# The spectrum steps of a fused four-layer kernel one to a slot, and at its beginning the input tiles ahead of the padded copy

## The chip, the cores and the metric

One core of a Trainium2 chip runs the whole program. The metric is the device time of one execution in microseconds (us), the median of several. Engines are called as the profile calls them: PE (TensorE), DVE (VectorE), ACT (ScalarE), POOL (GpSimd) and SP (SyncE, which here only issues DMAs; POOL issues DMAs too).

## The reference

Sixteen images of 224 x 224 pixels and 32 channels go through four residual layers, `x = x + layer(groupnorm(x))`. Only layers 0 and 1 are touched here.

```python
x = x + _L0_conv_ref(_gn(x), L0_conv_W, L0_conv_b, 224)  # offsets dy, dx = clip(mean(x) @ W + b, 0, 28);
                                                         # the image shifted by (dy, dx), zeros moved in
x = x + _L1_conv_ref(_gn(x), L1_conv_W, L1_conv_b)       # sign(x) * (sum over m of sign(W[m])), 3x3, SAME
x = x + _L2_conv_ref(_gn(x), ...)                        # 32 x 32 Fourier/cosine modes mixed, back, + x @ W.T, relu
x = x + _L3_conv_ref(_gn(x), ...)
```

Layer 2 begins with a cosine transform over columns and a Fourier transform over rows of each image, of which 32 x 32 modes are kept. These forward transforms are already worked out in the pass over layers 0 and 1, and stored in `spec`.

## The kernel before

`shift_conv_forward` does layers 0 and 1 and layer 2's forward transforms. The engines run in order, each its own list, and meet by semaphores only. The order is written out by hand.

Before the loop, image 0 is read in 16 tiles (`load_x`: of each, SP loads the two upper quarters of the partitions and POOL the two lower). DVE turns each tile into the image buffer (`turn_x`), and ACT sums it and its squares (`x_tile`); a ring of 4 tile buffers (`RING`) is between. From the sums come the mean, the variance and the offsets, which SP and POOL read from the tile `offi`. The shifted image is then read with the offset in its address. For image 0 that can reach ahead of the input, so its first 8 shifted tiles are read from `xpad`, a copy of the image's upper part with 29 rows of zeros ahead of it (L353 zeros, L355 copy). `pad_done` counts those DMAs. DVE also prepares the convolution's kernel sums (L722 to L743).

After that, `body(b, ...)` runs for b = -1 to 15, and each engine has its own version of it. A body has 16 slots. In it image b is convolved (`has_v`), image b+1 gets its shifted tiles added (`has_s`), image b+2 is read and its statistics are taken (`has_x`), and the spectrum of image b-1 is finished (`has_tail`). The steps of a slot s are

- PE: `conv(b, s)`, 18 matmuls into one of two PSUM pairs `cps`; `turn_back(b, s-1)`, 8 transposes in two halves into the two banks `aps`; every other slot `forward_cols` (tile `vps`)
- DVE: `add_conv(b, s)` (L846), which waits for the conv and frees its PSUM pair; `turn_x` (L812) for image b+2; `add_shifted` (L823 to L838) for image b+1; now and then `signs` (L870)
- ACT: `copy_back` (L618), the two halves from `aps` to `tout`; `square` (L649); `x_tile` (L600, L606) for each tile that DVE turned one slot earlier, four instructions of two tiles in slots 1 to 3
- SP and POOL: the loads of the tiles, four tiles ahead of DVE.

The spectrum of image b-1 is 8 steps. Step k of `spectrum` on PE is `forward_rows(k-1)` (L535, needs ACT's copy of step k-1) and `turn_spec(k)` (L524, 4 transposes into `aps[k % 2]`). ACT then copies that bank to `colpart` (`copy_cols`, L636). The banks `aps` are shared with `turn_back`: `ring_item` makes PE wait before it writes a bank until ACT has copied what stood in it two items earlier. `ring_t` and `ring_o` number the items of a body. After step 7 ACT copies the result (`copy_spec`) and SP stores it in eight DMAs (`store_spec`). PE's `conv(b, s+1)` stands behind `turn_back(b, s-1)` and slot s's spectrum steps.

A body whose flags are all set runs for b = 1 to 13 (13 bodies, 12 of them in a loop of four turns over three); b = 14 and b = 15 have less of DVE's work.

## Time and profile before

| | us |
|---|---|
| median of 3 runs | 3697.39 (3688.41 to 3705.35) |
| the profiled execution | 3689.45, span of its instructions 3687.8 |
| first tile turned | 60.77 |
| first convolution added (body 0) | 180.5 |
| body 0 | 93.9 |
| bodies 1 to 13 | 1370.1, 105.4 each |
| body 14 | 84.3 |

A body is counted from the first `add_conv` on DVE to the next body's. The profiler's own execution is one of several, and layers 2 and 3 fill the rest of the span. In the rows below a wait stands in brackets or behind a bar, with what ended it.

### The profile page before, as it was taken

What the parts mean: (1) busy time and instruction counts of PE and PEld (TensorE: products, weight loads), DVE (VectorE), ACT (ScalarE), POOL (GpSimd) and SP (SyncE); (2) the same over time, 40 slices, a digit from 0 to 9 for tenths busy, and PEclk for the clock granted to TensorE, in tenths of its full rate; (3) what the DMA queues carried; (4) which work ended last, traced back from release to release, by engine and by line L of the source; (5) the groups of instructions that cost most, each with busy time, mean ns of one, the idle gap of its engine ahead of it and who ended that gap; (6) DMA issues with size and microseconds to landing.
All of it is one profiled execution on the core that took longest, in us unless ns stands there. A gap on an engine that the chain in (4) does not pass through costs nothing. (4 is left out here: it accounts for less than half of the span.)

```text
span 3687.8 us, 59833 instructions
## 1 busy us (share of the span) xinstructions
PE 3025.0 (82%) x17264; PEld 1403.7 (38%) x17264; DVE 2731.0 (74%) x3908; ACT 1507.8 (41%) x2728; POOL 553.4 (15%) x1059
## 2 busy tenths in 40 slices
PE   0189888888899888899847888888888727999997
PEld 0034444443344444444444333333333316444443
DVE  3897887888878788886144776767676642999998
ACT  3476766676767666764352222222222223000000
POOL 2333322233233233321010000000000010000000
PEclk9988887897888888889767999999999857999998
DMA  5676665676676666764176555454545255999998
GB/s 148 174 228 211 203 195 184 205 223 204 204 215 199 185 199 207 223 188 133 70 140 274 235 201 235 200 235 200 236 199 237 114 120 170 343 384 388 386 379 296
DMA packets 255824, 808.76 MB, mean 219 GB/s; under 512 B 85466, under 2 KB 119774, under 8 KB 244724
## 3 DMA queue, kind: packets, MB, share of 16 engines
q1 hardware_dynamic: 163796, 370.64, 30.8%
q10 hardware_dynamic: 58368, 316.72, 22.0%
q0 software_dynamic: 33376, 118.13, 11.3%
q8 instruction: 115, 1.88, 0.2%
q14 instruction: 169, 1.38, 0.1%
HBM read 479.39 MB, written 329.56 MB: 219 GB/s over the span
## 5 line engine op out<-in xcount | busy, mean ns | idle before, releaser
L969 POOL DMA_DIRECT2D A_rin<-in_x x1008 | 507.4, 504 | 1151.6 <-DVE A_image L812 532.3
L1482 ACT ACTIVATE B_junk<-B_im,B_nk 128x896 bf16<-128x896 f32 x224 | 232.8, 1039 | 744.9 <-DVE B_im L1540 610.3
L472 PE MATMUL A_cps<-A_sign,A_cfull 128*128 128x448 bf16 x1344 | 409.8, 389 | 5.4 <-issue 5.4
L1733 PE MATMUL C_ring<-C_im,C_wnorm 128*128 128x448 f32 x896 | 387.8, 571 | 24.4 <-DVE C_ubuf L1790 19.4
L1400 PE MATMUL B_ring<-B_rout,b_k_rowf 128*64 128x512 f32 x896 | 306.6, 774 | 118.3 <-DVE B_rout L1533 118.3
L846 DVE SCALAR_TENSOR_TENSOR A_image<-A_cps,A_cbias,A_image 128x896 f32<-128x896 f32 x224 | 256.9, 1147 | 190.5 <-PE A_cps L472 187.3
L1428 PE MATMUL B_ring<-B_im,B_wnorm 128*128 128x448 f32 x896 | 384.9, 571 | 7.1 <-DVE B_wnorm L1511 4.8
L500 PE MATMUL A_aps<-a_k_ident,A_image 128*112 128x128 f32 x1792 | 286.6, 306 | 115.6 <-DVE A_image L846 85.2
L1540 DVE SCALAR_TENSOR_TENSOR B_im<-B_ring,B_im 128x896 f32<-128x896 f32 x224 | 239.1, 1085 | 183.8 <-PE B_ring L1438 182.2
L477 PE MATMUL A_cps<-A_sign,A_cedge 32*32 32x448 bf16 x1344 | 369.6, 384 | 0.0
L479 PE MATMUL A_cps<-A_sign,A_cedge 32*32 32x448 bf16 x1344 | 369.4, 384 | 0.0
L618 ACT ACTIVATE A_tout<-A_aps 112x512 f32<-112x512 f32 x448 | 247.3, 590 | 295.4 <-PE A_aps L500 190.4
L823 DVE STREAM_TRANSPOSE A_moved<-A_rin 128x896 f32<-128x896 f32 x256 | 282.3, 1103 | 64.3 <-DMA A_rin<-in_x 43.4
L500 PEld LDWEIGHTS A_aps<-a_k_ident,A_image 128*112 128x112 f32 x1792 | 237.6, 187 | 223.9 <-issue 150.5
L812 DVE STREAM_TRANSPOSE A_image<-A_rin 128x896 f32<-128x896 f32 x256 | 275.3, 1098 | 59.8 <-DMA A_rin<-in_x 32.2
L511 PE MATMUL A_vps<-A_tout,a_k_dctj 112*32 112x512 f32 x896 | 267.4, 727 | 20.1 <-ACT A_tout L618 20.1
L838 DVE SCALAR_TENSOR_TENSOR A_image<-A_moved,A_lin,A_image 128x896 f32<-128x896 f32 (+1 forms) x256 | 265.0, 1035 | 9.1
L1799 DVE STREAM_TRANSPOSE C_rout<-C_im 128x2048 f32<-128x2048 f32 (+1 forms) x128 | 259.3, 2028 | 5.8 <-DMA out<-C_rout 4.1
L1533 DVE STREAM_TRANSPOSE B_rout<-B_im 128x2048 f32<-128x2048 f32 (+1 forms) x128 | 256.4, 2024 | 0.0
L600 ACT ACTIVATE A_junk<-A_image 128x896 bf16<-128x896 f32 (+1 forms) x256 | 219.6, 858 | 81.5 <-DVE A_image L812 71.2
L1428 PEld LDWEIGHTS B_ring<-B_im,B_wnorm 128*128 128x128 f32 x896 | 160.5, 189 | 239.5 <-issue 208.5
L606 ACT ACTIVATE A_junk<-A_image,A_nx 128x896 bf16<-128x896 f32 (+1 forms) x256 | 243.0, 949 | 8.5
(198 smaller groups left out, 3720.7 us busy)
## 6 DMA issues: line engine op xcount, KB each, us to landing
A_rin<-in_x POOLq DMA_DIRECT2D x1008, 112.0 KB, 3.8
A_rin<-in_x SPq DMA_DIRECT2D x1008, 112.0 KB, 3.6
x2s<-A_image ACTq DMA_DIRECT2D x112, 896.0 KB, 4.8
B_im<-x2s SPq DMA_DIRECT2D x112, 896.0 KB, 10.1
x3s<-B_im ACTq DMA_DIRECT2D x112, 896.0 KB
C_im<-x3s SPq DMA_DIRECT2D x112, 896.0 KB, 13.1
out<-C_rout ACTq DMA_DIRECT2D x192, 256.0 KB
out<-C_rout ACTq DMA_DIRECT2D x192, 192.0 KB
```

The source lines that it names most:

```text
L472: return nc.tensor.matmul(banks[:, s, 0:LPN], cfull[:, tap, :], lines(n, s, slice(0, P), 0, tap), start=(tap == 0), stop=(tap == 2), skip_ ...
L477: nc.tensor.matmul(banks[bottom, s_top, 0:LPN], cedge[top, tap, :], lines(n, s_top, top, -1, tap), start=False, stop=False, skip_group_che ...
L479: nc.tensor.matmul(banks[top, s_bottom, 0:LPN], cedge[bottom, tap, :], lines(n, s_bottom, bottom, 1, tap), start=False, stop=False, skip_g ...
L500: last = nc.tensor.transpose(aps[side][0:HR, l * P:(l + 1) * P], image[q][:, first:first + 2 * HR].rearrange("p (j s) -> p s j", s=2)[:, l ...
L511: last = nc.tensor.matmul(vps[32 * g:32 * g + 32, :], con["k_dctj"][:, half, :], tout[G % OUTS][:, half, :], start=(half == 0), stop=(half ...
L812: nc.vector.transpose(turned_view(image[q], SECOND * t, ch * CHQ, CHQ), flat_view(rin[slot][:, :])).then_inc(tile_turned, 1)
L823: nc.vector.transpose(moved[:, :].rearrange("p (l q s) -> p q l s", q=CHQ, s=2), flat_view(rin[at_tile % RING][:, :])).then_inc(tile_turne ...
L838: nc.vector.scalar_tensor_tensor(out=dst, in0=m[:, lo:16, :], scalar=lin[:, 0:1], in1=dst, op0=ALU.mult, op1=ALU.add, accum_out=addsum[:, ...
L969: pool.dma_start(rin[slot][32 * i:32 * i + 32, :], rows[:, first * C:(first + CHQ) * C]).then_inc(in_lower[slot], 16)
L1400: last = nc.tensor.matmul(bank[64 * side:64 * side + 64, hq, :], con["k_rowf"][:, t, :], rout[p % 2][:, t, q0:q0 + BANK], start=(t == 0), ...
L1428: nc.tensor.matmul(slot(par, ("add", e))[:, lane % 2, 0:2 * SIZE], wnorm[par][:], im[par][:, EVN * e:EVN * (e + 1)].rearrange("p (m s) -> ...
L1733: nc.tensor.matmul(slot(add_place(e))[:, lane % 2, 0:2 * SIZE], wnorm[par][:], im[par][:, EVN * e:EVN * (e + 1)].rearrange("p (m s) -> p s ...
```

## The change

It has two parts.

At the beginning, the 14 DMAs that write zeros become one with the same bytes (each of 29 rows, 2 KB in size, 14 to a row), the 16 tiles of image 0 are issued next, and the copy of the image into `xpad` follows them. SP and POOL wait for `pad_done` only before they read the first offset. DVE's kernel sums move from the very beginning to behind the eighth tile.

In the bodies, the spectrum's steps spread out. Before, slots 0 to 3 have two steps each (one ahead of `turn_back`, one behind it) and slot 4 has the last `forward_rows`. Now slots 0 to 7 have one each, ahead of `turn_back`, but for slot 3, which keeps two. `copy_spec` moves from slot 5 to 8, `store_spec` from 6 to 9, `image_statistics` from 3 to 10, and the first `copy_rows` from the end of slot 5 to behind `copy_back` in slot 6.

```diff
-            return (3 + 4 * n if n < 3 else 8 + 2 * n) + half
+            return ((2, 5, 8, 12, 15, 18)[n] if n < 6 else 8 + 2 * n) + half
+
+        def spec_step(s):
+            return s if s < 4 else s + 1
         def ring_t(k):
-            return (0, 1, 2, 5, 6, 9, 10, 13)[k]
+            return (0, 1, 4, 7, 10, 11, 14, 17)[k]
...
# SP
-            for g in range(SIZE * C // BANK):
-                sp.dma_start(xpad[0:29].rearrange("r q c -> r (q c)")[:, g * BANK:(g + 1) * BANK],
-                             zrow).then_inc(pad_done, 16)
-            sp.dma_start(xpad[29:29 + P] ..., x[0, 0:P] ...).then_inc(pad_done, 16)
+            sp.dma_start(xpad[0:29].rearrange("r q c -> r (q c)").rearrange("r (g f) -> r g f", f=BANK),
+                         zrow.unsqueeze(1).to_broadcast([29, SIZE * C // BANK, BANK])).then_inc(pad_done, 16)
...
-            sp.wait_ge(pad_done, 16 * (SIZE * C // BANK + 1))
+            sp.dma_start(xpad[29:29 + P] ..., x[0, 0:P] ...).then_inc(pad_done, 16)
...
                         if k == 0:
+                            if isinstance(b, int) and b == -1:
+                                sp.wait_ge(pad_done, 32)
                             sp.wait_ge(off_ready, b + 2)
...
-                    if has_tail and s == 6:
+                    if has_tail and s == 9:
                         store_spec(b - 1)
# PE
-                    if has_tail and s < 5:
-                        spectrum(b - 1, 2 * s, ring_base(b))
+                    if has_tail and s < 8:
+                        spectrum(b - 1, spec_step(s), ring_base(b))
...
-                    if has_tail and s < 4:
-                        spectrum(b - 1, 2 * s + 1, ring_base(b))
+                    if has_tail and s == 3:
+                        spectrum(b - 1, 4, ring_base(b))
# ACT: copy_cols in the same places as spectrum; and
+                    if has_v and s == 6:
+                        copy_rows(b, 0)
-                    if has_tail and s == 5:
+                    if has_tail and s == 8:
                         copy_spec(b - 1)
...
-                    if has_v and s in (5, 9, 13):
+                    if has_v and s in (9, 13):
                         copy_rows(b, (s - 5) // 4)
# DVE
+                if k == 7:
+                    kernel_sums()
...
-                    if has_tail and s == 3:
+                    if has_tail and s == 10:
                         image_statistics(b - 1, far)
```

SP's list at the beginning, before (`A_rin` is the ring of tiles, `A_image` holds the zeros):

```order
L349 UNCONDITIONAL_BRANCH
L353 DMA xpad<-A_image 29x512 x14
L355 DMA xpad<-in_x 64x14336
L362 DMA A_rin<-in_x 32x896 x36
L402 TENSOR_LOAD A_offi
L402 ISA x2
L403 TENSOR_LOAD A_offi
```

and now:

```order
L353 UNCONDITIONAL_BRANCH
L356 DMA xpad<-A_image 406x1x512
L363 DMA A_rin<-in_x 32x896 x32
L390 DMA xpad<-in_x 64x14336
L363 DMA A_rin<-in_x 32x896 x4
L406 TENSOR_LOAD A_offi
L406 ISA x2
```

Thirty-two of the 36 tile loads, image 0's, have moved ahead of the copy `xpad<-in_x`, and the store of zeros is one DMA of 406 pieces.

DVE's list at the beginning now, from the last preparations on (L818 turns tiles, L738 to L751 are the kernel sums, L763 begins the statistics):

```order
L734 MEMSET A_sign 128x3192
L818 STREAM_TRANSPOSE A_image<-A_rin 128x28x16x2
L756 TENSOR_REDUCE A_sm<-A_image 128x1
L757 TENSOR_SCALAR A_nx<-A_sm 128x1
L818 STREAM_TRANSPOSE A_image<-A_rin 128x28x16x2 x7
L738 TENSOR_SCALAR A_image<-A_image 128x1152
L739 TENSOR_TENSOR A_image<-A_image 128x576
L740 TENSOR_TENSOR A_image<-A_image 128x288
L741 TENSOR_SCALAR A_image<-A_image 128x288
L742 TENSOR_REDUCE A_image<-A_image 128x32
L744 COPY A_image<-A_image 128x32 x3
L749 CAST A_cfull<-A_image 32x3x32 x10
```

The kernel sums stood ahead of the first of these tiles, and now stand between the eighth and the ninth.

PE's list in slot 2 of a full body, before, from the end of one convolution to the beginning of the next (L472 the convolution, L535 and L524 a spectrum step, L500 the two halves of `turn_back`):

```order
L472 MATMUL A_cps<-A_sign,A_cfull 128x448 x2
L528 REGISTER_ALU
L535 MATMUL A_wps<-A_colpart,a_k_fwdr 64x128 x4
L432 REGISTER_ALU
L524 MATMUL A_aps<-a_k_ident,A_rowspec 64x128 x4
L493 REGISTER_ALU
L500 MATMUL A_aps<-a_k_ident,A_image 112x128 x4
L432 REGISTER_ALU
L500 MATMUL A_aps<-a_k_ident,A_image 112x128 x4
L535 MATMUL A_wps<-A_colpart,a_k_fwdr 64x128 x4
L524 MATMUL A_aps<-a_k_ident,A_rowspec 64x128 x4
L472 MATMUL A_cps<-A_sign,A_cfull 128x448 x2
```

and now, with its new line numbers (L476, L539 and L528, L504):

```order
L476 MATMUL A_cps<-A_sign,A_cfull 128x448 x2
L539 MATMUL A_wps<-A_colpart,a_k_fwdr 64x128 x4
L436 REGISTER_ALU
L528 MATMUL A_aps<-a_k_ident,A_rowspec 64x128 x4
L497 REGISTER_ALU
L436 REGISTER_ALU
L504 MATMUL A_aps<-a_k_ident,A_image 112x128 x4
L436 REGISTER_ALU
L504 MATMUL A_aps<-a_k_ident,A_image 112x128 x4
L476 MATMUL A_cps<-A_sign,A_cfull 128x448 x2
```

The second step, behind `turn_back`, is gone from this slot; the first one stays.

ACT's list, before, from the last square of slot 1 over the beginning of slot 2 (L636 copies a spectrum bank, L618 the halves of `turn_back`):

```order
L606 ACTIVATE A_junk,A_xsq<-A_image,A_nx 128x896
L631 REGISTER_ALU
L633 REGISTER_ALU
L636 ACTIVATE A_colpart<-A_aps 64x512
L618 ACTIVATE A_tout<-A_aps 112x512
L615 REGISTER_ALU
L618 ACTIVATE A_tout<-A_aps 112x512
L631 REGISTER_ALU
L633 REGISTER_ALU
L636 ACTIVATE A_colpart<-A_aps 64x512
```

and now, the same place:

```order
L610 ACTIVATE A_junk,A_xsq<-A_image,A_nx 128x896
L635 REGISTER_ALU
L637 REGISTER_ALU
L640 ACTIVATE A_colpart<-A_aps 64x512
L619 REGISTER_ALU
L622 ACTIVATE A_tout<-A_aps 112x512
L619 REGISTER_ALU
L622 ACTIVATE A_tout<-A_aps 112x512
L625 REGISTER_ALU
```

The second copy of a spectrum bank has moved to later slots. The first one still stands behind the squares of the slot before.

## Rows read from the trace of the kernel before

**Rows 1.** Stretches of image 0 and of images 1 to 13, in us
```profile
core 0: us, PE busy (x) PEld busy (x) DVE busy (x) ACT busy (x) POOL busy (x), PEclk, DMA share, GB/s
180.50:274.40 93.90, 80.65 (x428) 32.43 (x426) 85.14 (x153) 65.69 (x128) 33.14 (x66) 0.86 0.74 229
274.40:1644.50 1370.10, 1220.42 (x6837) 560.51 (x6838) 1123.66 (x2065) 926.12 (x1768) 415.55 (x825) 0.84 0.66 203
```

**Rows 2.** Timeline of the beginning: start, us, engine, line, tiles, [idle before <-releaser]
```profile
7.47 29.32 SPq L353 DMA_DIRECT2D xpad<-A_image  x14
...
21.14 0.76 DVE L722 TENSOR_SCALAR A_image<-A_image 128x1152 f32<-128x1152 f32 x1 [13.70 <-DMA A_b0s<-in_L_conv_b]
...
24.24 0.35 DVE L728 COPY A_image<-A_image 128x32 f32<-128x32 f32 x3
...
33.49 1.98 DVE L741 CAST A_cfull<-A_image 32x96 bf16<-32x96 f32 x10
...
36.83 3.81 SPq L355 DMA_DIRECT2D xpad<-in_x  x1
...
60.77 1.11 DVE L812 STREAM_TRANSPOSE A_image<-A_rin 128x896 f32<-128x896 f32 x1 [23.71 <-DMA A_rin<-in_x]
...
77.84 1.11 DVE L812 STREAM_TRANSPOSE A_image<-A_rin 128x896 f32<-128x896 f32 x1 [0.49 <-DMA A_rin<-in_x]
...
95.75 0.17 DVE L757 TENSOR_REDUCE A_sm<-A_xsum 128x1 f32<-128x16 f32 x1 [9.95 <-ACT A_junk L606]
...
102.89 0.17 DVE L798 CAST A_offi<-A_sm 128x2 int32<-128x2 f32 x1
```

**Rows 3.** DMA issues up to 60 us: the stores of zeros, KB each
```profile
xpad<-A_image SPq DMA_DIRECT2D x14, 58.0 KB
```

**Rows 4.** Two stretches of the beginning, columns as in Rows 1
```profile
24.00:36.00 12.00, 0.15 (x1) 0.15 (x1) 9.90 (x24) 0.00 (x0) 0.00 (x0) 1.00 0.07 25
56.00:60.00 4.00, 0.00 (x0) 0.00 (x0) 0.00 (x0) 0.00 (x0) 0.00 (x0) 1.00 0.06 22
```

**Rows 5.** Groups of DVE in images 1 to 13: busy, mean ns | idle before <-releasers
```profile
L823 DVE STREAM_TRANSPOSE A_moved<-A_rin 128x896 f32<-128x896 f32 x208 | 229.3, 1102 | 50.0 <-DMA A_rin<-in_x 35.9 <-DVE A_sm L771 7.1 <-DVE A_mv L762 5.1
...
L846 DVE SCALAR_TENSOR_TENSOR A_image<-A_cps,A_cbias,A_image 128x896 f32<-128x896 f32 x182 | 208.6, 1146 | 129.3 <-PE A_cps L472 126.3 <-DVE A_sm L852 2.8
```

**Rows 6.** DVE's timeline, slots 2 to 5 of image 5
```profile
724.74 1.15 DVE L846 SCALAR_TENSOR_TENSOR A_image<-A_cps,A_cbias,A_image 128x896 f32<-128x896 f32 x1 [5.64 <-PE A_cps L472]
...
735.97 1.15 DVE L846 SCALAR_TENSOR_TENSOR A_image<-A_cps,A_cbias,A_image 128x896 f32<-128x896 f32 x1 [3.13 <-PE A_cps L472]
...
741.80 1.15 DVE L846 SCALAR_TENSOR_TENSOR A_image<-A_cps,A_cbias,A_image 128x896 f32<-128x896 f32 x1
```

**Rows 7.** PE's timeline, the same slots
```profile
715.91 0.98 PE L500 MATMUL A_aps<-a_k_ident,A_image 128*112 128x128 f32 x4 [1.94 <-ACT A_colpart L636]
...
719.57 0.95 PE L472 MATMUL A_cps<-A_sign,A_cfull 128*128 128x448 bf16 x2
...
724.63 1.97 PE L535 MATMUL A_wps<-A_colpart,a_k_fwdr 64*64 64x128 f32 x8
...
727.52 3.04 PE L511 MATMUL A_vps<-A_tout,a_k_dctj 112*32 112x512 f32 x8
...
731.57 1.08 PE L535 MATMUL A_wps<-A_colpart,a_k_fwdr 64*64 64x128 f32 x8
...
733.07 0.55 PE L472 MATMUL A_cps<-A_sign,A_cfull 128*128 128x448 bf16 x2
...
735.86 1.08 PE L535 MATMUL A_wps<-A_colpart,a_k_fwdr 64*64 64x128 f32 x8
```

**Rows 8.** ACT's timeline, slots 1 and 2 of image 5
```profile
709.77 1.03 ACT L649 ACTIVATE A_junk<-A_image,A_nk 128x896 bf16<-128x896 f32 x1
...
715.28 0.57 ACT L636 ACTIVATE A_colpart<-A_aps 64x512 f32<-64x512 f32 x1
```

**Rows 9.** Slots 0 to 3 of image 4, and 14 us of image 5
```profile
596.90:632.60 35.70, 33.45 (x189) 18.40 (x190) 23.98 (x42) 20.32 (x37) 10.71 (x21) 0.81 0.54 165
716.00:730.00 14.00, 14.00 (x54) 6.35 (x54) 7.86 (x19) 7.61 (x14) 3.63 (x7) 0.51 0.55 171
```

More of the change, by code:

```diff
@@ L351, in _ @@
             sp.wait_ge(setup, 1)
-            for g in range(SIZE * C // BANK):
-                sp.dma_start(xpad[0:29].rearrange("r q c -> r (q c)")[:, g * BANK:(g + 1) * BANK],
-                             zrow).then_inc(pad_done, 16)
-            sp.dma_start(xpad[29:29 + P].rearrange("r q c -> r (q c)"),
-                         x[0, 0:P].rearrange("r q c -> r (q c)")).then_inc(pad_done, 16)
+            sp.dma_start(xpad[0:29].rearrange("r q c -> r (q c)").rearrange("r (g f) -> r g f", f=BANK),
+                         zrow.unsqueeze(1).to_broadcast([29, SIZE * C // BANK, BANK])).then_inc(pad_done, 16)
             def load(flat, k, slot):
@@ L388, in _ @@
                 load_x(0, k, k % RING)
-            sp.wait_ge(pad_done, 16 * (SIZE * C // BANK + 1))
+            sp.dma_start(xpad[29:29 + P].rearrange("r q c -> r (q c)"),
+                         x[0, 0:P].rearrange("r q c -> r (q c)")).then_inc(pad_done, 16)
             def body(b, has_x, has_tail):
@@ L672, in body @@
                         copy_rows(b - 1, NSPEC - 1)
-                    if has_tail and s < 4:
-                        copy_cols(b - 1, 2 * s, ring_base(b) + ring_t(2 * s))
+                    if has_tail and s < 7:
+                        copy_cols(b - 1, spec_step(s), ring_base(b) + ring_t(spec_step(s)))
                     if has_v and 1 <= s <= UNITS:
                         copy_back(b, q, s - 1)
-                    if has_tail and s < 4:
-                        copy_cols(b - 1, 2 * s + 1, ring_base(b) + ring_t(2 * s + 1))
-                    if has_tail and s == 5:
+                    if has_v and s == 6:
+                        copy_rows(b, 0)
+                    if has_tail and s == 3:
+                        copy_cols(b - 1, 4, ring_base(b) + ring_t(4))
+                    if has_tail and s == 8:
                         copy_spec(b - 1)
@@ L719, in _ @@
             nc.vector.memset(zrow, 0.0).then_inc(setup, 1)
-            dve.wait_ge(wload, 16 * 7)
-            link(nc.vector.tensor_scalar(wraw, wraw, 0.0, None, ALU.is_ge))
-            link(nc.vector.tensor_tensor(wraw[:, 0:2], wraw[:, 0:2], wraw[:, 2:4], ALU.add))
-            link(nc.vector.tensor_tensor(wsum, wraw[:, 0], wraw[:, 1], ALU.add))
-            link(nc.vector.tensor_scalar(wsum, wsum, 2.0, -4.0, ALU.mult, ALU.add))
-            link(nc.vector.tensor_reduce(wtap[:, 0, :], wsum[:, :, :].rearrange("p t c -> p c t"), AX.X, ALU.add))
-            for g in range(1, QG):
-                nc.vector.tensor_copy(wtap[:, g, :], wtap[:, 0, :])
             nc.vector.memset(ones[:], 1.0)
@@ L736, in _, with kernel_sums @@
             link(nc.vector.memset(sign[1][:], 1.0))
-            w4 = wsum[:, :, :].rearrange("p (h w) c -> p h w c", w=3)
-            for i in range(QG):
-                rows = slice(32 * i, 32 * i + 32)
-                for o in range(max(0, i - 1), min(QG, i + 2)):
-                    nc.vector.tensor_copy(cfull[rows, :, 32 * o:32 * o + 32], w4[rows, i - o + 1, :, :])
-            nc.vector.tensor_copy(cedge[96:128, :, :], w4[96:128, 0, :, :])
-            nc.vector.tensor_copy(cedge[0:32, :, :], w4[0:32, 2, :, :]).then_inc(setup, 1)
-            dve.wait_ge(mean_out, 1)
-            link(nc.vector.tensor_copy(bias[:], mps[:, 0:1]))
+            def kernel_sums():
+                dve.wait_ge(wload, 16 * 7)
+                link(nc.vector.tensor_scalar(wraw, wraw, 0.0, None, ALU.is_ge))
+                link(nc.vector.tensor_tensor(wraw[:, 0:2], wraw[:, 0:2], wraw[:, 2:4], ALU.add))
+                link(nc.vector.tensor_tensor(wsum, wraw[:, 0], wraw[:, 1], ALU.add))
+                link(nc.vector.tensor_scalar(wsum, wsum, 2.0, -4.0, ALU.mult, ALU.add))
+                link(nc.vector.tensor_reduce(wtap[:, 0, :], wsum[:, :, :].rearrange("p t c -> p c t"), AX.X, ALU.add))
+                for g in range(1, QG):
+                    nc.vector.tensor_copy(wtap[:, g, :], wtap[:, 0, :])
+                w4 = wsum[:, :, :].rearrange("p (h w) c -> p h w c", w=3)
+                for i in range(QG):
+                    rows = slice(32 * i, 32 * i + 32)
+                    for o in range(max(0, i - 1), min(QG, i + 2)):
+                        nc.vector.tensor_copy(cfull[rows, :, 32 * o:32 * o + 32], w4[rows, i - o + 1, :, :])
+                nc.vector.tensor_copy(cedge[96:128, :, :], w4[96:128, 0, :, :])
+                nc.vector.tensor_copy(cedge[0:32, :, :], w4[0:32, 2, :, :]).then_inc(setup, 1)
             def guess(b, q):
@@ L895, in _ @@
                     guess(0, 0)
+                if k == 7:
+                    kernel_sums()
+            dve.wait_ge(mean_out, 1)
+            link(nc.vector.tensor_copy(bias[:], mps[:, 0:1]))
             for i in (0, 1, 2, 4, 3):
@@ L984, in _ @@
                 load_x(0, k, k % RING)
-            pool.wait_ge(pad_done, 16 * (SIZE * C // BANK + 1))
             def body(b, has_x):
@@ L995, in body @@
                         if k == 0:
+                            if isinstance(b, int) and b == -1:
+                                pool.wait_ge(pad_done, 32)
                             pool.wait_ge(off_ready, b + 2)
```

## The prediction

> **What bounds the kernel now.** I read three views, in this order: the stretches of the first layers' pass, then the timeline of the beginning, then one full body on three engines.
>
> The stretches show that body 0, which has no spectrum, takes 93.9 us, and that bodies 1 to 13 take 1370.1 / 13 = 105.4 us each with nearly the same DVE work (85.1 against 86.4 us) [rows 1]. So the spectrum costs 11.5 us per body, and the part of it that can be hidden is the prize.
>
> At the beginning the first tile is turned at 60.77 us, after DVE waited 23.7 us for a DMA; the sums of the 16 tiles end at 95.75, and the offset is there at 102.9 [rows 2]. Nothing else happens before 60.77, so all of it is on the path. From 24 to 36 us the DMA engines are 7% busy at 25 GB/s [rows 4]: one engine of 16, writing the zeros. They are 14 x 58 KB [rows 3] = 831 KB, which at 25 GB/s is 33 us. SP cannot issue the loads behind them: it issues zeros for 29.3 us and the copy for 3.8 more [rows 2]. From 56 to 60 again a single engine is at work (6%, 22 GB/s) [rows 4]: it ended its zeros last and now has its share of the copy ahead of its share of the tiles.
>
> In the bodies DVE waits 126.3 us for PE's convolution, 9.7 us per body [rows 5]. In image 5 that is 5.64 and 3.13 us before two additions, while the next follows after 5.8 us without a wait [rows 6]. PE's timeline shows why. PE waits 1.94 us in `turn_back`'s second half for ACT's spectrum copy, and then everything takes nearly twice as long: a convolution 5.1 us (719.57 to 724.63) against 2.8 (733.07 to 735.86), a spectrum step 2.9 against 1.5 (731.57 to 733.07) [rows 7]. From 716 to 730 the granted clock is 0.51, so nearly all of that stretch is at 1.2 GHz [rows 9]. ACT's copy was late because the square and two tiles stand ahead of it, 709.77 to 715.28 = 5.5 us [rows 8].
>
> **The beginning, worked out.** The one big store has the same 2 KB pieces. If one engine writes it, the zeros again take 33 us of that engine, the POOL loads beside them again stretch them, and SP is again held until about 37. The copy leaves the path: 128 rows of 28 KB = 3.67 MB, a sixteenth of it 229 KB, at 25 GB/s 9.2 us on that engine. With SP's 3.8 us for issuing it, partly in the same time, I take 10 us: the first tile at about 51. Bounds: 0 if the copy was not what delayed the tile, 18 if the zeros end at 8 + 33 = 41 and the tile follows in 2.
>
> The Trainium skill (DMA: Bandwidth & Descriptors, Why a DMA increments its semaphore by 16 and not by 1) says that a DMA uses the largest number of engines up to 16 that divides the slowest dimension on both sides. The trace agrees for 29 rows, at 7% of 16 engines [rows 4]. For 406 pieces against 29 rows it again gives one, so it speaks against a spread store.
>
> Everything behind shifts with the first tile, since ACT is busy without a break from there to 95.75. The kernel sums cost 3.5 us (21.14 to 24.59) and about 2.4 (the casts from 33.49 on, 1.98 and two small ones) [rows 2], 5.9 together, now between tiles 8 and 9. DVE is then some six us ahead of ACT (it turned the twelfth tile at 77.84, while ACT has 16 tiles in 34 us, 2.1 to 2.3 each). They are hidden, at worst 1 us. If that cover were gone, they would cost 5.9. The copy is issued once the twelfth tile is turned, 77.84 + 1.1 - 10 + 5 = 74, and with all engines takes about 11 us (9.2 and the latency), to 85 or 87. The offset is there at 102.9 - 10 = 92.9. So `pad_done` is met in time, by 6 us. Behind that wait on SP and POOL stand only the shifted loads, which need the offset anyway. The first two tiles of image 1 are behind the copy in SP's queue, and are not wanted before 94. Sum: **-10**.
>
> **The bodies, worked out.** PE's work is not less. A slot with one step is 2.8 + 1.5 + 1.0 (`turn_back`, 730.56 to 731.57) = 5.3 us at the full clock, against 5.8 of DVE [rows 6, 7]; with `forward_cols` (3.0 at the low clock, I take 1.9 at the high) it is 7.2. With two steps it was 6.8 and 8.7. Slots 0 to 2 get lighter by 1.5 each, slot 3 stays, slots 4 to 7 get heavier by 0.4 to 1.5. By PE's work alone the waits nearly vanish.
>
> But each step's bank stands ahead of `turn_back`, whose second half needs ACT's copy of it, and ACT's slot is 5.5 + 0.6 + 1.1 = 7.2 us where two tiles are in it [rows 8]. I follow the lists with these prices, time 0 at the first addition, DVE's slots 5.7 to 6.3. ACT ends slot 1 at 10.1; PE has done its half of `turn_back` at 8.8 and waits to 10.7, so the 1.9 us wait of [rows 7] is still there, in slot 2. ACT ends slot 2 at 18.3, slot 3 at 27.3. Then PE waits again (26.0 to 27.9, slot 4), where before `turn_back` had no spectrum bank ahead of it. Three outcomes for DVE's waits on PE in slots 1 to 8:
> - the clock stays up: 0.3 + 1.5 + 1.5 + 0.9 = 4.2 us
> - it falls once, behind the first wait, for 14 us: 5.4 + 1.5 + 1.5 + 0.7 = 9.1 us
> - it falls behind both waits: 9.1 + 6 = 15 us (a low stretch costs two convolutions 2.3 each and a step 1.4).
>
> Now it is 9.7 on the mean and 8.8 in image 5, with one fall. So in a body like image 5, one fall as before gives nothing, none gives 5, two cost 6. That averages to about 0 over nine bodies.
>
> Four bodies (the first of each turn of the loop) begin at the low clock, as image 4 does: 35.7 us for four slots at 0.81 [rows 9], against 23.6 of DVE's work. There the lighter slots 0 to 2 save two steps at 2.9 and one at 1.5 = 7.3, and give back 1.5 later: -5.8 x 4 = **-23**.
>
> `image_statistics` (1.5 us of DVE) moves to slot 10, where DVE often waits for a shifted tile (35.9 us of such waits over 13 bodies, 2.8 each [rows 5]); some 0.3 to 0.5 of it is hidden: **-5**. `store_spec`'s eight issues hold SP's next loads up in slot 10 instead of 7: nothing on balance, if that cover is gone 1 us x 13. Bodies 14 and 15 have PE at work throughout, with the same work: 0.
>
> Sum: 3689.5 - 10 - 23 - 5 = 3651.5. The profiled execution is 7.9 us under the median of the three runs and 1.0 over the fastest, so I forecast 3652, and the range covers the rest.
>
> **The rivals.**
> - *The clock stays up.* The wait in slot 2 is as long as now, but PE has less queued around it. Nine bodies gain 5 more: 3652 - 45 = 3607. For it: one spectrum step less in each of the light slots lets ACT begin earlier. Against: my sum has the same 1.9 us wait, and [rows 7, 9] show the low clock behind just such a wait.
> - *Slower: PE is now tied to ACT in slots 4 to 6 too.* The second wait lets the clock fall again. If that happens in all nine bodies, 9 x 6 = 54 more: 3706, and more if the four others do it too. It decides from some six bodies with two falls on, where it eats the 38 us of the rest. For it: ACT's 7.2 us slots against DVE's 5.8. Against: slots 4 and 5 have one tile each, so ACT catches up.
> - *The zeros are spread over the engines.* Then the first tile comes at about 20 us, and the beginning gives 41: 3652 - 31 = 3621. For it: the destination is 406 pieces, not 29 rows. Against: the source is still 29 rows.
> - *Nothing to see:* the gain of the beginning and the loss in slots 4 to 8 cancel, 3689 within 18.
>
> **How the numbers follow.** Chances: forecast 0.42 (3630 to 3675), clock up 0.22 (3585 to 3625), spread 0.06, no change 0.17, slower 0.13. Half a per cent, about what a measurement tells from no change, is 18 us. Faster 0.42 + 0.22 + 0.06 + a little of the fourth = 0.73; same 0.15; slower 0.12. The range leaves out the last tenth on either side: 3588 to 3702.
>
> **What the changed profile would show.** The first tile turned at 51 (20 if spread, 60 if the copy did not matter), and 7% of the DMA engines until 36. Offset at 93, with SP waiting for the offset, not for `pad_done`. DVE's wait for the convolution near 7 us per body instead of 9.7, and moved from slots 2 and 3 towards 4 to 6. PE's wait for ACT's spectrum copy in more than one slot of a body, and the clock's low stretches after those. Bodies 1 to 13 at 103.2 us. I am wrong if bodies are under 101 (the clock held) or over 105 (tied to ACT), or if `pad_done` comes last.

## The result, and the profile after

The changed kernel takes 3649.06 us (median of 4 executions, 3640.05 to 3669.61) against 3700.41 us before (4 executions). The ratio is 0.9875, 95% interval 0.9833 to 0.9917: it is faster by 1.2%. The forecast was 3652. Here and below a ratio leaves out executions more than 1.5% above the fastest of their kernel, 12 of before's 17 in the second set of experiments, so the ratios of that set lie nearer to 1 than its medians (for the changed kernel 0.990 against 0.980).

The execution that was profiled took 3669.61 us, 19.8 less than the profiled one before. The timeline of the beginning of the changed kernel answers to [rows 2]:

```profile
7.58 0.87 SPq L356 DMA_DIRECT2D xpad<-A_image  x1
8.50 62.95 SPq L363 DMA_DIRECT2D A_rin<-in_x  x32
...
49.94 1.11 DVE L818 STREAM_TRANSPOSE A_image<-A_rin 128x896 f32<-128x896 f32 x1 [33.51 <-DMA A_rin<-in_x]
...
61.03 0.72 DVE L738 TENSOR_SCALAR A_image<-A_image 128x1152 f32<-128x1152 f32 x1
...
66.45 0.20 DVE L751 CAST A_cedge<-A_image 32x96 bf16<-32x96 f32 x1
...
84.99 0.17 DVE L763 TENSOR_REDUCE A_sm<-A_xsum 128x1 f32<-128x16 f32 x1 [4.13 <-ACT A_junk L610]
...
92.13 0.17 DVE L804 CAST A_offi<-A_sm 128x2 int32<-128x2 f32 x1
```

SP issues the zeros in 0.87 us and is at the loads from 8.50 us on, and yet the first tile is turned at 49.94: 10.8 us earlier than before, not 30. Up to 12 us the same timeline shows one load only:

```profile
8.50 32.57 SPq L363 DMA_DIRECT2D A_rin<-in_x  x1
```

SP's first load of a tile holds it until 41.07, about when one engine is through with the zeros (8 + 33 us by the prediction's sum). So SP was not free earlier than before; it only stood in another instruction. The kernel sums lie between tiles 8 and 9 and the sums of the tiles end 10.8 us earlier, so ACT was not delayed by them. The first addition of image 0 is at 170.90, 9.6 earlier.

The stretches answer to [rows 1] and [rows 4]: image 0, images 1 to 13, and the wait at the beginning. Columns as there.

```profile
170.90:266.10 95.20, 81.35 (x429) 33.23 (x428) 85.28 (x152) 66.26 (x127) 32.76 (x66) 0.83 0.75 225
266.10:1652.85 1386.75, 1232.68 (x6837) 554.62 (x6836) 1123.48 (x2065) 929.84 (x1768) 417.36 (x828) 0.84 0.65 201
24.00:36.00 12.00, 0.00 (x0) 0.00 (x0) 0.00 (x0) 0.00 (x0) 0.00 (x0) 1.00 0.07 26
```

DMA is again 7% busy at 26 GB/s from 24 to 36 us. Two more stretches, the first of before, the second of the changed kernel:

```profile
41.00:51.00 10.00, 0.00 (x0) 0.00 (x0) 0.00 (x0) 0.00 (x0) 0.00 (x0) 1.00 1.05 369
```

```profile
46.00:50.00 4.00, 0.00 (x0) 0.00 (x0) 0.06 (x1) 0.00 (x0) 0.00 (x0) 1.00 0.07 26
```

Before, all engines moved 3.7 MB from 41 to 51 us: that is the copy, 10 us ahead of the tiles. The prediction saw the copy in the one engine at work from 56 to 60 us. The changed kernel has such a stretch right ahead of its first tile too, and no copy there, so it is more likely the late engine's share of the tiles (16 loads of 112 KB, a sixteenth of them, at 26 GB/s: 4.4 us, an estimate).

And images 1 to 13 are not shorter here: 1386.75 us against 1370.10. The groups of DVE in the same stretch, beside [rows 5], say where it waited:

```profile
L829 DVE STREAM_TRANSPOSE A_moved<-A_rin 128x896 f32<-128x896 f32 x208 | 229.0, 1101 | 47.3 <-DMA A_rin<-in_x 23.7 <-DVE A_sm L777 7.1 <-issue 6.0
...
L852 DVE SCALAR_TENSOR_TENSOR A_image<-A_cps,A_cbias,A_image 128x896 f32<-128x896 f32 x183 | 209.8, 1147 | 154.8 <-PE A_cps L476 151.8 <-DVE A_sm L858 2.8
```

151.8 us of waits for the convolution against 126.3. PE's group of the turned halves in the same stretches, before and now, has the wait for ACT's spectrum copy twice as long (11.1 us more of it stood at L535 before, none does now):

```profile
L500 PE MATMUL A_aps<-a_k_ident,A_image 128*112 128x128 f32 x1456 | 236.0, 309 | 104.9 <-DVE A_image L846 76.4 <-ACT A_colpart L636 26.4 <-ACT A_tout L618 1.9
```

```profile
L504 PE MATMUL A_aps<-a_k_ident,A_image 128*112 128x128 f32 x1456 | 235.9, 305 | 111.1 <-DVE A_image L852 56.0 <-ACT A_colpart L640 54.5
```

DVE's waits for the convolution have grown, and they stand elsewhere. Mean length of the slots 0 to 13 of images 1 to 13, each from one addition to the next, from the starts of the 14 additions of an image:

```
slot     0    1    2    3    4    5    6    7    8    9   10   11   12   13
before  6.7  7.5 10.5 10.5  5.8  6.3  6.0  6.7  6.6  5.1  6.3  6.7  6.8 13.9
after   5.6  6.0  7.2  9.3  9.0 10.0  6.0  6.3  6.0  5.5  8.3  6.7  6.8 14.0
```

Slots 0 to 3 gained 7.1 us, slots 4 and 5 gave back 6.9, and slot 10 grew by 2.0. The timelines of DVE, then PE, in slots 2 to 5 of image 4 show how (answers to [rows 6, 7]):

```profile
617.56 1.15 DVE L852 SCALAR_TENSOR_TENSOR A_image<-A_cps,A_cbias,A_image 128x896 f32<-128x896 f32 x1 [4.93 <-PE A_cps L476]
627.00 1.15 DVE L852 SCALAR_TENSOR_TENSOR A_image<-A_cps,A_cbias,A_image 128x896 f32<-128x896 f32 x1 [3.51 <-PE A_cps L476]
636.90 1.15 DVE L852 SCALAR_TENSOR_TENSOR A_image<-A_cps,A_cbias,A_image 128x896 f32<-128x896 f32 x1 [4.04 <-PE A_cps L476]
```

```profile
600.66 0.70 PE L504 MATMUL A_aps<-a_k_ident,A_image 128*112 128x128 f32 x4 [1.94 <-ACT A_colpart L640]
...
605.65 1.96 PE L539 MATMUL A_wps<-A_colpart,a_k_fwdr 64*64 64x128 f32 x8
...
608.53 3.63 PE L515 MATMUL A_vps<-A_tout,a_k_dctj 112*32 112x512 f32 x8
...
613.16 1.08 PE L539 MATMUL A_wps<-A_colpart,a_k_fwdr 64*64 64x128 f32 x8
...
621.58 0.70 PE L504 MATMUL A_aps<-a_k_ident,A_image 128*112 128x128 f32 x4 [2.02 <-ACT A_colpart L640]
...
626.89 1.96 PE L539 MATMUL A_wps<-A_colpart,a_k_fwdr 64*64 64x128 f32 x8
```

There are now two waits for ACT's spectrum copy, 1.94 us in slot 2 and 2.02 in slot 4, and behind each the same matmuls take twice as long: L539 1.96 us at 605.65, 1.08 at 613.16, and 1.96 again at 626.89. The stretches of this image give the granted clock:

```profile
588.74:599.37 10.63, 9.66 (x70) 5.25 (x66) 10.45 (x15) 6.30 (x12) 4.59 (x10) 1.00 0.59 180
599.37:610.00 10.63, 9.34 (x38) 3.83 (x40) 9.73 (x17) 8.39 (x16) 4.89 (x9) 0.62 0.93 288
...
617.50:637.00 19.50, 17.48 (x87) 7.68 (x87) 11.74 (x17) 12.04 (x24) 4.98 (x10) 0.74 0.52 166
637.00:661.00 24.00, 23.75 (x162) 11.19 (x162) 23.12 (x34) 21.73 (x46) 9.27 (x19) 1.00 0.75 229
```

It is 0.62 behind the first wait, 0.74 around the second and 1.00 ahead of the first and behind the second. Microsecond by microsecond it is 0.50, that is 1.2 GHz, from 602 to 612 us, and again from 623 to 630. Over images 1 to 13 PE waits for that copy 54.5 us, 0.4, 1.5 and 1.8 per image in slots 1, 2 and 4. Each of the 13 images has two waits of 1.4 us or more. Behind the second one the clock falls to 0.50 for about 10 us or more in 12 images; behind the first it does so in 5, for some 4 us in 2, and not at all in 6.

The two profiled executions differ by 19.8 us, but that can't be put down to the change. The unchanged pass of layer 2 alone differs by as much. The first row is before's, the second the changed kernel's:

```profile
1966.20:2985.20 1019.00, 888.26 (x3968) 349.62 (x3968) 698.00 (x817) 249.03 (x448) 1.97 (x4) 0.90 0.53 210
```

```profile
1964.90:2963.40 998.50, 867.68 (x3968) 345.40 (x3968) 697.02 (x817) 248.96 (x448) 1.97 (x4) 0.93 0.54 214
```

DVE's work is the same within 1 us; the granted clock is 0.90 and 0.93. So one profile of each could not tell what the change did in the bodies, and the experiments had to.

### The profile page after: what moved, and what is told of

The parts are those of the page before. It is cut to its first block and busy times, and to the rows that moved or that the text cites. A ratio compares the mean times of both kernels' runs of the same rounds, so it can differ in the third digit from the quotient of the medians.

```text
span 3668.0 us, 59821 instructions
## 1 busy us (share of the span) xinstructions
PE 3005.7 (82%) x17264; PEld 1386.8 (38%) x17264; DVE 2729.5 (74%) x3908; ACT 1511.8 (41%) x2728; POOL 554.2 (15%) x1059
## 5 line engine op out<-in xcount | busy, mean ns | idle before, releaser
L476 PE MATMUL A_cps<-A_sign,A_cfull 128*128 128x448 bf16 x1344 | 420.3, 397 | 6.6 <-issue 6.6
L504 PE MATMUL A_aps<-a_k_ident,A_image 128*112 128x128 f32 x1792 | 287.9, 303 | 127.8 <-DVE A_image L852 69.8
L1411 PE MATMUL B_ring<-B_rout,b_k_rowf 128*64 128x512 f32 x896 | 286.3, 725 | 118.4 <-DVE B_rout L1544 118.4
L481 PE MATMUL A_cps<-A_sign,A_cedge 32*32 32x448 bf16 x1344 | 379.7, 393 | 0.0
L483 PE MATMUL A_cps<-A_sign,A_cedge 32*32 32x448 bf16 x1344 | 379.5, 392 | 0.0
L504 PEld LDWEIGHTS A_aps<-a_k_ident,A_image 128*112 128x112 f32 x1792 | 237.4, 187 | 243.0 <-issue 133.3
L818 DVE STREAM_TRANSPOSE A_image<-A_rin 128x896 f32<-128x896 f32 x256 | 275.5, 1098 | 65.0 <-DMA A_rin<-in_x 49.8
```

Source lines behind the costliest of these rows:

```text
L476: return nc.tensor.matmul(banks[:, s, 0:LPN], cfull[:, tap, :], lines(n, s, slice(0, P), 0, tap), start=(tap == 0), stop=(tap == 2), skip_ ...
L481: nc.tensor.matmul(banks[bottom, s_top, 0:LPN], cedge[top, tap, :], lines(n, s_top, top, -1, tap), start=False, stop=False, skip_group_che ...
L483: nc.tensor.matmul(banks[top, s_bottom, 0:LPN], cedge[bottom, tap, :], lines(n, s_bottom, bottom, 1, tap), start=False, stop=False, skip_g ...
L504: last = nc.tensor.transpose(aps[side][0:HR, l * P:(l + 1) * P], image[q][:, first:first + 2 * HR].rearrange("p (j s) -> p s j", s=2)[:, l ...
L818: nc.vector.transpose(turned_view(image[q], SECOND * t, ch * CHQ, CHQ), flat_view(rin[slot][:, :])).then_inc(tile_turned, 1)
L1411: last = nc.tensor.matmul(bank[64 * side:64 * side + 64, hq, :], con["k_rowf"][:, t, :], rout[p % 2][:, t, q0:q0 + BANK], start=(t == 0), ...
```

## The experiments

Twelve runs, in three sets. The first (`begin_only`, `spread_only`, `turn_first`, `before_again`) ran on one chip, the second (`after_again`, `zeros16`, `best`, `order_only`) and the third (the other four) on another. Medians of before are 3713.29 us in the first set, 3722.91 in the second, 3704.94 in the third; each ratio is to before in its own set.

**Each part alone.** `begin_only` has the changed beginning and the spectrum as before, `spread_only` the reverse (with the moved statistics and stores). `begin_again` repeats the first.

> The beginning's part alone, the bodies as before. Theory A (the beginning gives its 10 us and nothing else, the rest of the 51 us measured comes from the bodies or is not real): first tile at 50 us, all 13 full bodies at 105.4 us, 3690 us, ratio 0.997. Theory B (the gain of 51 us hangs on the beginning, because everything behind it starts in another phase of the clock): ratio near 0.988. In the profile: the pass over layers 0 and 1 ends 10 us earlier than the 1834.6 us of before under A.

> The spread spectrum alone, the beginning as before. Theory A (bodies as in the profile of the changed kernel, 106.7 us against 105.4 each): the pass over layers 0 and 1 is 0 to 20 us longer, and the kernel is within 20 us of before, ratio 1.000 to 1.005. Theory C (my sum: waits of PE for ACT are moved, bodies gain 2 us each): ratio 0.993. If the 51 us come from here, it is 0.989.

> The beginning's part alone, a second time, since its first times (ratio 0.9896) gave 38 us where its profile moved the first tile by 10. Theory (the beginning is worth 10 us, the rest was the clock of those executions): ratio about 0.997, mean granted clock of its executions as before's, 0.868, first addition again at 169.9. Rival (the earlier beginning is really worth 20 to 38 us): ratio again 0.99 or less.

The beginning alone: 3677.62 us, ratio 0.9896 (0.9862 to 0.993), and the second time 3687.98, 0.9945 (0.9905 to 0.9984). Its profiles have the first tile turned at 50 and the first addition at 169.9 and 170.3, 10 us earlier. The spread alone: 3674.22, 0.9867 (0.9827 to 0.9907), first addition at 180.7, a larger gain than any of its three theories gave (0.989 at best). Each part makes the kernel faster by itself. The second run of the beginning holds the 10 us (0.27%) in its interval, the first doesn't.

**Before once more.** `before_again` is the kernel before, unaltered.

> The kernel before once more, for a second profile and for what two timings of one kernel differ by. If the pass of layer 2 (1019.0 us in the first profile of before, 998.5 in that of the changed kernel, with the same code) differs again by some 20 us from its first profile, that difference is one between executions and not the change's. If it is again 1019 within 3 us, the change reaches into layer 2's pass.

Ratio 0.9968 (0.9932 to 1.0003). That is the size of what identical kernels differ by here, and the second ratio of the beginning, 0.9945, is only 0.002 under it: that the beginning gives 10 us is shown by its traces, not by its times. Layer 2's pass took 994.2 us in this profile, so it differs between executions of one kernel. The profile also moves the base of the comparison. Stretch of images 1 to 13:

```profile
274.20:1665.59 1391.39, 1251.38 (x6836) 570.34 (x6837) 1124.57 (x2064) 927.27 (x1768) 416.72 (x828) 0.82 0.65 200
```

1391.39 against 1370.10 in [rows 1], for the same program: the execution on which the prediction was built had the shortest bodies of the four profiles with two steps per slot.

**The changed kernel twice more.** `after_again` and `after_third` are unaltered.

> The changed kernel unaltered, for a second set of times and a second profile. Theory (change moves the waits of the bodies and gains 10 us in the beginning, the rest of the 51 us is how layer 2's pass and the bodies fall from one execution to the next): ratio to before 0.985 to 0.992, beginning again 49.9 us to the first tile, bodies 1 to 13 between 1370 and 1400 us in sum, layer 2's pass at either 995 or 1019. Rival (the bodies really gain): bodies below 1365 in sum.

> The changed kernel unaltered, beside the others of this call, and for a third profile. Theory (one step per slot lets TensorE's clock stay up for more of the pass): mean granted clock of its executions 0.885 to 0.888 against 0.868 of before, ratio 0.985 to 0.99, bodies 1 to 13 at 1370 to 1387 us in sum. Rival (the higher clock of the earlier executions was chance): clock within 0.005 of before's.

3647.32 us, ratio 0.9899 (0.9846 to 0.9953), and 3650.42, 0.9823 (0.9762 to 0.9885). With the other variants there are now four profiles of the old list and six of the new one:

```
images 1 to 13, us             sum (granted clock)            waits for conv, per image
two steps: before              1370.1 (0.84)                   9.7
           before_again        1391.4 (0.82)                  11.8
           begin_only          1396.7 (0.82)                  11.6
           begin_again         1402.3 (0.82)                  12.1
one step:  after               1386.7 (0.84)                  11.7
           spread_only         1374.3 (0.84)                  10.3
           after_again         1385.2 (0.84)                  11.1
           after_third         1373.7 (0.84)                  10.6
           order_only          1363.6 (0.86)                   9.4
           zeros16             1360.2 (0.85)                   9.2
```

The means are 1390.1 and 1374.0: the new list makes the 13 bodies 16 us shorter, 1.2 each, and DVE's wait for the convolution goes from 11.3 to 10.4. The spread of one kind is up to 32 us, so 16 is a rough figure.

All executions, profiled or not, give their mean granted clock over the whole span. It is 0.869 for before (71 executions, before_again among them), 0.874 for the beginning alone (18), 0.885 for the spread alone (9), 0.887 for the changed kernel (22). So the higher clock comes with the spectrum's new list and was no chance; 0.005 of it comes with the beginning. Among executions of one program, time falls by 28 us per 0.01 of clock (slope within the groups). At an equal clock of 0.88 this line has before at 3679 us, the beginning alone at 3664, the spread alone at 3690, the changed kernel at 3667 to 3674. By it the new list costs some 5 to 11 us in added waits and is paid back by 0.013 to 0.016 of clock, 36 to 45 us. This is arithmetic on the means, not an experiment: a wait also changes the mean clock, and no run holds the one fixed while the other moves.

**ScalarE's copy ahead of the turned halves.** `turn_first` lets PE do `turn_back` first and the spectrum's step after it, ACT to match:

```
 PE, slot s:    conv(b, s)
-               spectrum(b - 1, spec_step(s))
                forward_cols
                turn_back(b, q, s - 1)
+               spectrum(b - 1, spec_step(s))
 ACT, slot s:
-               copy_cols(spec_step(s))
                copy_back; root; square
+               copy_cols(spec_step(s))
                the x tiles
```

> Everything of the change, but in each slot turn_back goes ahead of the spectrum step on PE, and ACT copies the spectrum bank behind its square and ahead of the tiles. Theory A (PE waits in turn_back for ACT's spectrum copy, and those waits let the clock fall): PE's wait for ACT's spectrum copy ahead of turn_back, 1.5 us in slot 2 and 2.0 in slot 4 of a body, is gone; the clock stays high in slots 2 to 5; DVE's wait for the convolution falls from 11.5 us per body to 5 or less; bodies at 99 to 101 us instead of 106.7, and the kernel 75 to 100 us under the changed one. Rival (PE's own work in slots 3 to 5 is what DVE waits for, at either clock): bodies stay at 104 to 107.

3566.09 us, ratio 0.9593 (0.9554 to 0.9632): some 82 us under the changed kernel's medians of 3647 to 3650 (from the other sets and the other chip, where before differs by 8 to 10 us). Stretch of images 1 to 13, then its groups of PE and DVE:

```profile
262.43:1550.21 1287.78, 1158.95 (x6845) 547.17 (x6844) 1122.92 (x2064) 915.15 (x1769) 415.76 (x825) 0.88 0.70 216
```

```profile
L504 PE MATMUL A_aps<-a_k_ident,A_image 128*112 128x128 f32 x1456 | 224.3, 303 | 63.4 <-DVE A_image L852 61.7 <-ACT A_tout L622 1.7
...
L539 PE MATMUL A_wps<-A_colpart,a_k_fwdr 64*64 64x128 f32 x832 | 120.1, 287 | 11.8 <-ACT A_colpart L640 11.8
```

```profile
L852 DVE SCALAR_TENSOR_TENSOR A_image<-A_cps,A_cbias,A_image 128x896 f32<-128x896 f32 x182 | 208.6, 1146 | 47.6 <-PE A_cps L476 44.6 <-DVE A_sm L858 2.8
```

The wait for the copy ahead of the turned halves, 54.5 us, is gone from L504, and 11.8 us of it are left at L539. The clock is 0.88, and DVE's waits fall from 151.8 to 44.6 us. Theory A holds in the wait, the bodies (99.1 us each) and the total. Where the low clock lies, from the granted clock of every microsecond of images 1 to 13:

```
us at 1.2 GHz per image   slots 0, 1   2, 3   4, 5   6 to 8   9 to 13    sum
before                         5.6      9.2    0.0     0.1      18.6    33.5
before_again                   9.4      9.6    0.0     0.1      19.7    38.8
after                          2.9      4.4   11.0     0.0      16.4    34.7
after_third                    2.2      4.5   10.1     0.0      16.9    33.7
turn_old (below)               5.9     10.5    0.0     0.0      18.5    34.9
turn_first                     4.4      3.0    1.4     0.0      14.3    23.1
```

In slots 2 to 5 it falls from 15.4 us in the changed kernel to 4.4. This shows the cause: PE does the same work in another order, and with the tie to ACT most of the low clock of these slots goes, and 86 to 99 us of the bodies. The run doesn't part what the waits cost themselves from what the low clock costs; by the line above, `turn_first` at a clock of 0.88 stands at 3628, so each is about half. In all six rows about half of the low clock or more lies in slots 9 to 13, where PE waits for DVE, up to 6.5 us at a time in the changed kernel; no run was made for that part. Slots 4 and 5 are 6.5 and 7.1 us long instead of 9.0 and 10.0.

**Is the spread needed for that?** `turn_old` has the changed beginning and the old two steps per slot, both behind `turn_back`:

```
 PE, slot s:    conv(b, s)
                forward_cols
                turn_back(b, q, s - 1)
+               spectrum(b - 1, 2 * s)
+               spectrum(b - 1, 2 * s + 1)
```

> The beginning's part with the spectrum's two steps per slot of before, but with both steps behind the slot's turned halves on TensorE, and ScalarE's two copies behind its square. Theory (the gain of turn_first comes from taking ScalarE's spectrum copy out of the chain that leads to the next addition, the even spread is needed only so that no slot is heavy): the wait ahead of the turned halves is gone, but slots 1 to 3 stay heavy, so about half of turn_first's gain, ratio 0.975 to 0.985. Rival (the spread is worth nothing, only the order counts): ratio as turn_first, 0.96. Other rival (only the spread counts): ratio as the beginning alone, 0.99.

3706.60 us, ratio 1.0006 (0.9974 to 1.0038): none of the three expectations holds. It is 19 us slower than the beginning alone in the same set, while the same move with one step per slot gained 80. The group of the spectrum's second half in images 1 to 13, and slot 2 of image 5:

```profile
L535 PE MATMUL A_wps<-A_colpart,a_k_fwdr 64*64 64x128 f32 x832 | 129.3, 303 | 50.1 <-ACT A_colpart L636 50.1
```

```profile
716.21 1.08 PE L535 MATMUL A_wps<-A_colpart,a_k_fwdr 64*64 64x128 f32 x8
718.30 0.62 PE L524 MATMUL A_aps<-a_k_ident,A_rowspec 128*64 128x128 f32 x4 [1.01 <-ACT A_tout L618]
720.28 1.94 PE L535 MATMUL A_wps<-A_colpart,a_k_fwdr 64*64 64x128 f32 x8 [1.36 <-ACT A_colpart L636]
```

With two steps in a row PE needs ACT's copy of the first within the same slot. The wait isn't removed but moved from `turn_back` to L535, with a new one for `copy_back`, and the next matmuls again take 1.94 us instead of 1.08. Only with one step per slot has a copy a whole slot of time. The spread alone is worth 1.3%, the order alone nothing, and the two with the beginning 4%.

**The statistics of the image.** `stats_back` is the changed kernel with `image_statistics` in slot 3 again; `store_spec` stays in slot 9.

> The changed kernel with the image's statistics back in slot 3, the rest as changed. Theory (they cost their whole time where they stand, slot 3 or slot 10): within 8 us of the changed kernel on the same chip, slot 10 shorter by 1 to 2 us per body, slot 3 longer by 1.5. Rival (slot 10 hid some of them behind a shifted tile, as predicted): slower by 5 us. Second rival (in slot 10 they delay the shifted tiles, and cost more than there): faster by 10 us or more.

3655.30 us, ratio 0.9845 (0.9788 to 0.9903), within 5 us of `after_third` in the same set. Slot 10 is not shorter (8.0 us in both). DVE's and SP's timelines in slots 9 and 10 of image 5:

```profile
751.65 1.15 DVE L852 SCALAR_TENSOR_TENSOR A_image<-A_cps,A_cbias,A_image 128x896 f32<-128x896 f32 x1
...
755.38 1.11 DVE L829 STREAM_TRANSPOSE A_moved<-A_rin 128x896 f32<-128x896 f32 x1 [2.57 <-issue]
...
759.54 1.11 DVE L829 STREAM_TRANSPOSE A_moved<-A_rin 128x896 f32<-128x896 f32 x1 [2.09 <-issue]
```

```profile
745.66 4.43 SPq L382 DMA_DIRECT2D spec<-A_specout  x8
750.42 11.29 SPq L363 DMA_DIRECT2D A_rin<-in_x  x12
```

Where the statistics stood, DVE is idle ahead of two shifted tiles, 2.57 and 2.09 us. The view names no releaser there ("issue"); that it waits for their loads is a reading of SP's timeline. Images 1 to 13 take 1353.0 us, 20.7 less than in `after_third`. That is within the spread of one kind, but also under all six in the table. So in slot 10 the statistics cost nothing that shows, and in slot 3 the wait for the convolution hides most of them (0.6 us there instead of 2.5). Which place is better by a few us these runs can't say. Slot 10's length has another cause. The rows point to `store_spec`: its eight issues hold SP for 4.43 us directly ahead of the loads that slot 10 wants. That wasn't tried by itself.

**The zeros on all engines.** `zeros16` writes the same zeros as one store whose both sides have 16 rows:

```
-xpad[0:29] as "r (g f)", f=512          <- zrow.to_broadcast([29, 14, 512])
+xpad[0:29] as "(p g f)", p=16, f=448    <- zrow[0:16, 0:448].to_broadcast([16, 29, 448])
```

> The changed kernel with one edit: the same zeros as one store whose both sides are 16 rows of 29 pieces of 1792 bytes. Theory (the zeros are slow because one DMA engine writes them, and both SP's issuing and the first tile wait for that engine): DMA engines well over 7% busy before 24 us, the first tile turned at 17 to 22 us instead of 49.9, offset at 60 to 65, total 28 to 32 us under the changed kernel, ratio to before about 0.978. Rival (the loads of the window's tables and POOL's rows are the limit, or the zeros cost the same whoever writes them): first tile at 40 or later, total within 10 us of the changed kernel.

3636.43 us, ratio 0.9854 (0.9753 to 0.9956). Stretches of its beginning, and its first tile:

```profile
12.00:16.00 4.00, 0.00 (x0) 0.00 (x0) 3.27 (x2) 0.00 (x0) 4.00 (x9) 1.00 0.94 118
...
20.00:24.00 4.00, 0.00 (x0) 0.00 (x0) 0.00 (x0) 0.00 (x0) 0.00 (x0) 1.00 1.06 212
```

```profile
25.19 1.11 DVE L818 STREAM_TRANSPOSE A_image<-A_rin 128x896 f32<-128x896 f32 x1 [8.85 <-DMA A_rin<-in_x]
```

The DMA engines are fully busy instead of 7%, and the first tile comes at 25.19 instead of 49.94, the first addition at 146.0 instead of 170.9. So it was the one engine that held the tiles. The expected 17 to 22 us is missed by three, and the offset comes at 67.4 instead of 60 to 65; the engines are full until the first tile, with zeros and tables and tiles, and the rows don't part them. The Trainium skill (DMA: Bandwidth & Descriptors, Why a DMA increments its semaphore by 16 and not by 1) would have a slowest dimension of 16 on both sides use 16 engines, and 29 only one. The trace agrees with both. The 24 us in the trace are 11 in the medians of one set, where 28 to 32 were expected; with 6 and 12 executions that lie up to 54 us apart, these times can't tell 11 from 24.

**Order or merging.** `order_only` is the changed kernel with the zeros as 14 stores, as before.

> The changed kernel with the zeros as 14 stores of one group each, as before, instead of one; the tiles still ahead of the copy. Theory (the copy ahead of the tiles cost the 10 us, the merging nothing): SP issues zeros for some 29 us again, the tiles' loads behind them, first tile at 49 to 52 us, total within 10 us of the changed kernel. Rival (the merged store gave part of it, since SP is free sooner): first tile at 54 us or later.

3643.03 us, ratio 0.9889 (0.9792 to 0.9985). SP issues zeros for 28.97 us again, and the first tile is turned at 49.40. The 10 us come from putting the tiles ahead of the copy; the merged store gives nothing, as SP's held first load above also says.

**Both together.** `best` is `turn_first` with the zeros of `zeros16`.

> turn_first (TensorE's two turned halves ahead of the spectrum's step, ScalarE's copies ordered to match) together with the zeros on 16 engines. Theory: the two are in different stretches, so they add: 0.9593 less 30 us of 3700, ratio 0.951, some 3520 us. Rival (the gain of the beginning is eaten by a clock that falls otherwise): 0.955 to 0.965.

3553.13 us, ratio 0.9658 (0.9572 to 0.9743). That is the lowest median of all, 94 us under the changed kernel's in the same set, and 13 under `turn_first`'s of another set. The expected 3520 us and 0.951 aren't reached. Its first addition is at 146.2, images 1 to 13 take 1293.1 us. The first tile gained its 24 us here too; the interval is too wide to say how much of it arrives at the end.

## Why the prediction was right, and where it wasn't

**The beginning, -10:** right in the trace, in size and in cause. One engine wrote the zeros again (7%, 26 GB/s), SP was held again (until 41.07, forecast 37), the copy's 10 us left the path, the first tile came at 49.94 (forecast 51), the offset at 92.13 (92.9), and the kernel sums, 5.6 us between tiles 8 and 9, were hidden. SP and POOL load the shifted tiles at 94.31 and 95.21, right behind the offset. Wrong was only the reading of the one engine from 56 to 60 us as the copy's. The times of the beginning alone gave 36 and 17 us in medians. Nothing in its profiles shows more than 10 to the first addition. By the line of clock, 15 of the 29 us between the means of `before` and the beginning alone stand at an equal clock and 14 go with 0.005 of clock; why the clock is higher there stays open.

**The bodies, -28 with the statistics:** the direction was right, the account behind it mostly not. The prediction named a sign of being wrong, "over 105 (tied to ACT)", and the changed profile shows it: 1386.75 / 13 = 106.7 us instead of 103.2; the mean of the six profiles is 105.7. The profiles show 16 us on the mean, while the spread alone gave 39 us in medians and 0.9867 as a ratio. The steps:
- Low stretches moved from slots 2 and 3 to 2 to 5, and PE waits for ACT in slots 2 and 4 (1.94 and 2.02 us in image 4): as worked out (1.9 each).
- Wrong: "that averages to about 0 over nine bodies", from one fall giving nothing, none 5 and two costing 6. Of these nine bodies four have two falls, four have one and one has none. So the three cases were a fair guess, but the price wasn't: slots 4 and 5 cost 6.9 us per body on the mean.
- The step that failed is the -23 for the four bodies that begin at the low clock. They do begin there, and their slots 0 to 3 gained 7.5 us each, as worked out (7.3). But they were to give back 1.5 later, and slots 4 and 5 took 6.6 each, since the second wait and its fall are in them too: with slot 10 the four together are only 1.3 us shorter. In the other nine the light slots pay as well (7.1 us on the mean of all 13), and yet these nine are 17.8 us longer in this pair of profiles. Over ten profiles the 13 bodies gain 16 us.
- `image_statistics`, -5: mis-sized. Moving them gave nothing that the times show. The 2.8 us of waits for shifted tiles per body, taken as their cover, were those of all slots; slot 10 had 1.2 of them.
- `store_spec`, "nothing on balance": it looks wrong. Slot 10 grew by 2.0 us, 26 over 13 bodies, and slots 7 and 8, which it no longer precedes, gave back 1.0. The bound of 1 us per body was too low, and slot 10 was counted as cover for the statistics and not as a place that loses its own loads.
- Wrong as a base: 9.7 us of waits per body before. That was the lowest of four profiles with two steps per slot, whose mean is 11.3.

So the forecast of 7 us of waits missed (11.7 in this profile, 10.4 over six). That 3652 lies 3 us from 3649 is in good part luck: the forecast took 38 us off 3689.5, a low execution of before, and the measured change took 51 off a median of 3700.4. The base was too low and the gain too small by about the same amount, and part of the gain came by a mean clock that rose over the whole span, which no term of the sum has.

**The rivals.** *Slower by the tie to ACT* had its mechanism right: the tie is there in most bodies, and `turn_first` shows that it costs 80 us. Yet the slots that got lighter pay for it. Its price, 6 us in each body with a second fall, is what slots 4 and 5 cost (6.9); what it counted too low is what the lighter slots pay in all bodies. *The clock stays up* didn't happen; it is nearly what `turn_first` does (0.88 over the bodies). *Zeros spread* didn't happen, and `zeros16` gave its mechanism.

**Open:** where in the span the clock of the timed executions is higher. Of the 0.016, the bodies can give 0.38 x 0.020 = 0.008 (mean clock 0.825 to 0.845 over 38% of the span, from the ten profiles). The rest isn't placed.

## What to carry to other kernels

When a step is spread evenly over slots, look for the other engine's copy between its halves and give it a whole slot, with work that needs no copy between them: the order alone was worth nothing here, the spread alone 1.3%, both (with the beginning) 4%. Before a profile is the base for a few per cent, take it twice and compare the parts that don't change. For a DMA that is slow for its bytes, look at the share of busy engines before its place in the queue: a share of 0.07 cost 24 us of the wait for the first tile, the order 10.

## What the runs showed of the hardware

- The pass of layer 2, the same code in all runs, took 1019.0 us at a granted clock of 0.90 in one profile of before and 994.2 at 0.93 in another. Most images of it take 61.4 us in the one, and 58.4, 58.7 or 60.4 in the other. `turn_first`, the second fastest kernel, had the slow form (1016.6 us).
- Behind a wait of PE of 1.94 us, which ended at 600.66, the granted clock was 0.50 (1.2 GHz) from 602 to 612 us; ahead of the wait it was 1.00. Such a wait doesn't always do it: of the 26 waits of 1.4 to 2.1 us for ACT's copy in images 1 to 13 of `after`, 19 had the low clock behind them and 7 had not, among them one of 2.12 us.
- With the zeros (812 KB) on one DMA engine, SP's next load, of 112 KB, held SP for 32.57 us (`after`). With the same zeros on 16 engines, SP issued 32 loads in 38.91 us and the first tile came 24.75 us earlier (`zeros16`).
- Eight store issues of 32 KB took SP 4.43 us, 0.55 each.
